# Expert rows loaded three slots ahead in the state-space stage, and 77 and 94 expert blocks in place of 80 and 96

## The chip, the core and the metric

The kernel runs on one core of a Trainium2 chip. The metric is the device time of one execution in microseconds (us); lower is better. The core has five engines that run side by side and wait for each other through semaphores: TensorE (PE), VectorE (DVE), ScalarE (ACT), GpSimd (POOL) and SyncE (SP), which here does nothing but wait and issue transfers. An engine works through its own instructions strictly in order, so a wait in SP's program also holds back every transfer that stands behind it.

## What is computed

Two layers over x of shape (2, 2048, 256), 4096 tokens in all, everything in float32. Layer 0 is a gated linear attention with a dense MLP, then a mixture of experts: each token goes to 2 of 14 experts (hidden 176) beside a shared one. Layer 1 is a state-space block (48 heads of 64, state 128, a causal convolution of four taps over 3072 channels) whose output is added to its input, then a mixture of 16 experts (hidden 96), again 2 for each token:

```
# layer 1, state space, for each token
h = exp(A * dt) * h + B (x) x ;  y = h . C + D * x
out = (rms(y) * silu(z)) @ out_proj.T ;  x = x + out
# experts, for each token t
for e in top2(t): out[t] += w[t, e] * (silu(x[t] @ wg[e].T) * (x[t] @ wu[e].T)) @ wd[e].T
```

In this kernel the experts of both layers are worked out before the state-space stage, and the sums of the second batch half are completed inside that stage.

## The kernel before

**The stages.** `layer0` (attention, MLP, routing of the first experts), `experts` (first mixture), `front` (what the state-space stage needs, and the second routing), `experts1` (second mixture), `ssm` (state space and the last sums). They follow one another with a barrier between.

**Expert blocks.** The routed rows (two for each token) are sorted by expert and each expert's rows are padded to whole blocks of 128. `experts` walks over NB = 80 blocks; `experts1` over 2 × NB1 = 96, 48 for each batch half of 2048 tokens. Which expert a block belongs to is read from a table, so the number of blocks is fixed at build time, and blocks behind the last one with rows in it do work whose result goes to rows that nobody reads. A block is: load of 128 rows (SP), transposes, gate and up projection, transposed hidden rows, down projection (PE), the splits into high and low parts and the gating between them (ACT, DVE), and an indirect DMA that sends the rows home (POOL). Blocks overlap: in a beat k the engines work on block k+2's transposes, block k's projections, block k-1's hidden rows and block k-2's result. While it walks, `experts` also clears the sorted rows of the second mixture (96 transfers of 128 rows from SP, spread over the blocks behind the fourth). In `experts1` the second half of the blocks also carries 16 groups that add the first half's expert rows to the sums, one for every second block from `FIRST = NB1 + 10` on.

**The state-space stage.** It runs N = 192 slots: 8 steps of 512 tokens, and 24 channel tiles in each. In slot k PE projects tile k (lines 63 to 65: bank X first, then bank Z), does the scores and the state update of tile k-1 (L2501, L2509), reads the state of tile k-2 (L2518), projects tile k-4 out (again L63 to L65), and transposes tile k (L2556). DVE does `to_end(k-1)` (L2823), `convolve(k)` (L2755, then three times L2761, on bank X), `gate(k)` (L2767), `silu(k)` (L2772), `scan(k-1)` (eight times L2803), `own_tokens(k-1)` (L2810) and, last of the slot, `state_part(k-2)` (L2817). POOL does L2678 twice and L2684, L2691, L2695, L2705 once each. So L2755 marks the start of a slot on DVE, and below a slot is counted from its L2755 to the next one's. In the slots with t = 4 (k = 28, 52, 76 and so on) DVE first scales and adds the finished step's output (`evacuate`), ahead of L2755, so the slot before (27, 51, 75) is the long one.

**The pieces.** Slots 6 to 37 (K0 = 6, 32 slots) each carry a piece: one of the two expert rows of 128 tokens of the second batch half. PE transposes it into bank X once the taps of this slot are done (`row_turned`, L2526), DVE adds bank X to the sum of these 128 tokens (`row_added`, L2780), and only then may PE project the next slot into bank X. Two pieces (c = 0 and 1) make a unit u of 128 tokens: its sum `part_acc` is loaded before the first and stored after the second.

**SP's program.** It sets the order of the transfers. For each k: `weights_in(k+2)` (L2388), `log_decay(k+2)` (L2393), `since_start(k+1)` (L2401, which waits for `t1` of tile k-2, that is for L2817, DVE's last instruction of slot k), `weights_out(k-1)` (L2405), then `keep_part` (L2429) if the piece of slot k-2 closed a unit, then `expert_row` (L2421 and, for c = 0, L2425) for the piece of slot k+1. Inside `expert_row` the load of the sum waits for the store of the unit two before:

```
done(sp, "row_turned", i - 2)
sp.dma_start(row[:, i % 2], ...)
if c == 0:
    if u >= 2:
        sp.wait_ge(ph[f"part_kept{u % 2}"], u // 2 * 16)
    sp.dma_start(part_acc[:, u % 2], ...)
```

At k = 2u+9 `keep_part(u)` is issued and right behind it, in the same k, the load of unit u+2, which waits for that store to land. The row tiles (two) and the sums (two) lie in columns of the constant table `tab` that this stage no longer uses, so in the profile a row load is `tab<-expert_scratch`, a sum's load `tab<-acc_scratch` and its store `acc_scratch<-tab`.

Of the kernel before, what the change touches and what calls it, by code (L numbers as in the profile page):

```python
# [13 lines left out]
P = 128  # L14
# [13 lines left out]
IN0, SH0, IN1 = 176, 352, 96  # L28
NB, NB1 = 80, 48

HM, PH, NST = 48, 64, 128
# [67 lines left out]
def program(nc, xT, table, gla_w, gla_wo, wbc, moe0, ffn0, moe1, mamba, a_dram, outT):  # L99
    ctx = ExitStack()  # L100
    with ctx:
# [63 lines left out]
        with ExitStack() as own:  # L165
# [5 lines left out]
            experts1(nc, pool, bank, moe1, down_drams[1], sorted1_dram, out1_dram, acc_dram, disp1, home[:, B * T // P:], swdge, x_all, col)  # L171
        ssm(nc, pool, bank, mamba, wi_dram, wo_dram, a_drams, ea_drams, dec_dram, acc_dram, out1_dram, f_dram, outT, st, vec_dram, swdge, col)

# [1098 lines left out]
def experts(nc, pool, bank, moe0, down_dram, sorted_dram, sorted1_dram, out_dram, disp, swdge, col):  # L1272
# [5 lines left out]
    with ExitStack() as own:  # L1278
# [57 lines left out]
        with ExitStack() as blocks:  # L1336
# [18 lines left out]
            def has(n):  # L1355
                return 0 <= n < NB

            def rows(n):
                return slice(n * P, (n + 1) * P)

            BEATS = range(-2, NB + 3)
            NCLEAR = sorted1_dram.shape[0] // P
            with nc.Block(no_gpsimd_drain=True) as block:

                @block.sync
                def _(sp):
                    for n in range(NB):
                        done(sp, "xt", n - RX)
                        done(sp, "spot", n - RX)
                        sp.dma_start(x[:, n % RX], sorted_dram[rows(n)]).then_inc(ph[f"x{n % RX}"], 16)  # L1370
                        if n == RX:
                            sp.wait_ge(ph["zeros"], 1)
                        if n >= RX:
                            m = n - RX
                            for i in range(m * NCLEAR // (NB - RX), (m + 1) * NCLEAR // (NB - RX)):
                                sp.dma_start(sorted1_dram[rows(i)], zeros[:]).then_inc(ph["cleared"], 16)
                    sp.wait_ge(ph["cleared"], NCLEAR * 16)

                @block.gpsimd
                def _(pl):  # L1380
                    for n in range(NB):
                        done(pl, "y", n)
                        pl.indirect_dma_start(out_dram[:], bass.IndirectOffsetOnAxis(ap=home[:, n % RH, :], axis=0),  # L1383
                                              y[:, n % RO], None).then_inc(swdge[f"home0{n % RO}"], 16)
                    for r in range(RO):
                        pl.wait_ge(swdge[f"home0{r}"], NB // RO * 16)

                @block.tensor
                def _(pe):
# [41 lines left out]

                    for k in BEATS:
                        if has(k + 2):
                            turn(k + 2)
                        if has(k):
                            gate_up(k)
                        if has(k + 1) and (k + 1) % EL == 0:
                            n = min(EL, NB - k - 1)
# [92 lines left out]
def front(nc, pool, bank, wbc, acc_dram, rows_out, sorted_dram, f_dram, a_drams, ea_drams, dec_dram, home, disp1, swdge,  # L1531
# [6 lines left out]
    with ExitStack() as own:  # L1538
# [50 lines left out]
        with nc.Block(no_gpsimd_drain=True) as block:  # L1589
# [247 lines left out]
            def _(dve):  # L1837
# [7 lines left out]
                for k in BEATS:  # L1845
# [100 lines left out]
                    if bb is not None:  # L1946
                        done(dve, "ranks", bb)
                        js = slice(bb * NG, (bb + 1) * NG)
                        if bb:
# [7 lines left out]
                               {"place": disp1["place"][:, :, js], "weight": x_all[:, js, D + 2:D + 4].rearrange("p g c -> p c g"),  # L1957
                                "expert": disp1["expert"][:, bb * NB1:(bb + 1) * NB1],
                                "of_block": disp1["of_block"][:, bb * NB1:(bb + 1) * NB1]})
        ph.clear()  # L1960


def experts1(nc, pool, bank, moe1, down_dram, sorted_dram, rows_out, acc_dram, disp1, partition, swdge, x_all, col):
# [4 lines left out]
    GU, HH, Q = 2 * IN1, IN1, 8  # L1968
    N = B * NB1
    NG = NS * NJ  # L1970
# [10 lines left out]
    with ExitStack() as own:  # L1981
# [108 lines left out]
        with nc.Block(no_gpsimd_drain=True) as block:  # L2090

            @block.sync
            def _(sp):
                def expert_rows(u):
                    if u == 0:
                        for n in range(NB1 - RO, NB1):
# [15 lines left out]
                for k in range(-2 - RX, N + 3):  # L2112
                    n = k + 2 + RX
                    if has(n):
                        if n == NB1:
# [114 lines left out]
            def _(pl):  # L2230
# [8 lines left out]
                for r in range(RO):  # L2239
                    pl.wait_ge(swdge[f"home1{r}"], N // RO * 16)  # L2240

# [69 lines left out]

def ssm(nc, pool, bank, m_dram, wi_dram, wo_dram, a_drams, ea_drams, dec_dram, acc_dram, rows_out, f_dram, outT, st, vec_dram, swdge, col):

    with ExitStack() as own:
# [44 lines left out]
        def has(g):  # L2361
            return 0 <= g < N
# [19 lines left out]
        with nc.Block(no_gpsimd_drain=True) as block:  # L2382

            @block.sync
            def _(sp):
# [30 lines left out]
                def expert_row(i):  # L2416
                    u, c = i // 2, i % 2
                    ts = slice(u * P, (u + 1) * P)
                    a = FIRST_ROW + 2 * (T + u * P)
                    done(sp, "row_turned", i - 2)  # L2420
                    sp.dma_start(row[:, i % 2], rows_out[a:a + 2 * P].rearrange("(p c) d -> p c d", c=2)[:, c, :]).then_inc(ph[f"row{i % 2}"], 16)  # L2421
                    if c == 0:
                        if u >= 2:
                            sp.wait_ge(ph[f"part_kept{u % 2}"], u // 2 * 16)
                        sp.dma_start(part_acc[:, u % 2], acc_dram[1, :, :, ts]).then_inc(ph[f"part{u % 2}"], 16)  # L2425

                def keep_part(u):
                    done(sp, "row_added", 2 * u + 1)
                    sp.dma_start(acc_dram[1, :, :, u * P:(u + 1) * P], part_acc[:, u % 2]).then_inc(ph[f"part_kept{u % 2}"], 16)  # L2429

                def sums(s):
                    done(sp, "kept", s - 1, 16)
                    if s == NS:
                        for r in range(2):
                            sp.wait_ge(ph[f"part_kept{r}"], NU // 2 * 16)
                    sp.dma_start(acc[:], acc_dram[s // NS, :, :, step(s)]).then_inc(ph["acc"], 16)
# [19 lines left out]
                sp.dma_start(chain[:, 0], m_dram[:, :, MP_ST:MP_W].rearrange("t p c -> p t c")).then_inc(ph["init"], 16)  # L2456
                for k in range(0, N + 1):
                    if has(k + 2):
                        weights_in(k + 2)
                        log_decay(k + 2)  # L2460
                    if has(k + 1):
                        since_start(k + 1)
                    if has(k - 1):
                        weights_out(k - 1)
                    if piece(k - 2) is not None and piece(k - 2) % 2:
                        keep_part(piece(k - 2) // 2)
                    if piece(k + 1) is not None:
                        expert_row(piece(k + 1))
                    s, t = k // NCT, k % NCT
# [13 lines left out]
            def _(pe):  # L2483
# [37 lines left out]
                def row_turned(k):  # L2521
                    i = piece(k)
                    pe.wait_ge(ph[f"row{i % 2}"], (i // 2 + 1) * 16)
                    done(pe, "tap", k, NR)
                    for h in range(KD):
                        o = pe.transpose(bank[:, X, h * P:(h + 1) * P], row[:, i % 2, h * P:(h + 1) * P], col("ident"))  # L2526
                    o.then_inc(ph["row_turned"], 1)
# [222 lines left out]
            def _(dve):  # L2750
# [23 lines left out]
                def row_added(i):  # L2774
                    u = i // 2
                    if i % 2 == 0:
                        dve.wait_ge(ph[f"part{u % 2}"], (u // 2 + 1) * 16)
                    done(dve, "row_turned", i)
                    done(dve, "row_added", i - 1)
                    dve.tensor_tensor(part_acc[:, u % 2], bank[:, X, 0:D].rearrange("p (k t) -> p k t", k=KD), part_acc[:, u % 2], ALU.add)\  # L2780
                        .then_inc(ph["row_added"], 1)
# [180 lines left out]
```

## Time and profile before

| | us |
|---|---|
| median of 3 executions | 3188.53 (3184.73 to 3191.90) |
| the profiled execution's own time | 3188.92 |
| its span, first to last instruction | 3187.1 |
| PE, DVE, ACT, POOL busy over the span | 2725.0, 2393.8, 2133.6, 1980.3 |

Lines of the profile name the source line, the engine and the tiles (written `out<-in`). In a timeline the first two numbers are the start and the duration in us, and a bracket at the end tells how long the engine stood idle before the instruction and what ended that. "Releaser" is the instruction or transfer for which it waited. SPq is SP's sequencer issuing a transfer. The clock in the rows is the granted clock of TensorE as a share of full speed.

### The profile page before, as it was taken

Reading aid. Unit: us, or ns where it says so; the run is one execution under the profiler, and the core shown is the slowest. Engines: PE = TensorE matmul, PEld = TensorE weight load, DVE = VectorE, ACT = ScalarE, POOL = GpSimd, SP = SyncE. Lnnn points to the kernel's source line nnn. Section 1 sums busy time; section 2 is a strip of 40 time slices with the busy share of each in tenths; the row PEclk is TensorE's granted clock in tenths of the full one; section 3 lists DMA queues with packets and bytes.
Section 4 is the critical chain, followed back from the end, with each engine's and each line's share of the span. In section 5 each row is a group of like instructions: output and inputs, shape, how many; then the busy total and the mean of one; then the engine's idle time right before and its main releaser. Section 6 shows DMA issues by size and latency. Waiting matters only on the chain.

```text
span 3187.1 us, 58909 instructions
## 1 busy us (share of the span) xinstructions
PE 2725.0 (86%) x17390; PEld 2136.2 (67%) x17390; DVE 2393.8 (75%) x6012; ACT 2133.6 (67%) x4702; POOL 1980.3 (62%) x1702
## 2 busy tenths in 40 slices
PE   3699888985569887378788889999999999999998
PEld 2366666654459765277566667788787878878786
DVE  2466666663377588558677778999899999999996
ACT  3454455432255466345576668999899999999996
POOL 2222221216224314554477678999999999999998
PEclk9699998997879998689899999999999999999999
DMA  5455554545656554447765566676766667666663
GB/s 131 111 180 168 170 175 163 183 134 179 201 177 195 173 161 155 148 130 219 216 202 175 171 195 206 199 227 200 241 203 208 218 199 226 201 213 211 197 215 123
DMA packets 321372, 589.70 MB, mean 185 GB/s; under 512 B 48022, under 2 KB 139574, under 8 KB 320566
## 3 DMA queue, kind: packets, MB, share of 16 engines
q1 hardware_dynamic: 306470, 545.73, 55.6%
q0 software_dynamic: 14592, 40.19, 3.4%
q8 instruction: 150, 2.46, 0.3%
q14 instruction: 160, 1.31, 0.1%
HBM read 465.11 MB, written 124.83 MB: 185 GB/s over the span
## 4 chain that ended last, share of the span: by engine, by line
POOL 28%; issue 8%; DMA 5%; DVE 4%; ACT 2%; SPq 2%; PE 1%; POOLq 0%; DVEq 0%; ACTq 0%
POOL mm L2678 6%; POOL y L2691 6%; POOL y_lo L2684 6%; POOL yz L2695 5%; POOL y L2705 5%; DMA tab<-expert_scratch 2%; DMA acc_scratch<-tab 2%; DVE part L2803 2%; SPq L2401 1%; DMA tab<-acc_scratch 1%; ACT mt L2608 1%; DVE t L2817 1%; DVE cv L2761 1%; SPq L2405 1%; DVE t L2810 1%
## 5 line engine op out<-in xcount | busy, mean ns | idle before, releaser
L2678 POOL TENSOR_TENSOR mm<-mt,cb 128x512 f32<-128x512 f32 x384 | 489.6, 1298 | 60.4 <-ACT mt L2628 58.1
L2608 ACT ACTIVATE mt<-a_wide,a_tok 128x128 f32<-128x128 f32 x1536 | 487.0, 389 | 3.5 <-POOL mm L2678 2.8
L2761 DVE SCALAR_TENSOR_TENSOR cv<-bank,taps,cv 128x509 f32<-128x509 f32 (+2 forms) x576 | 429.4, 745 | 13.6
L63 PE MATMUL bank<-f,wi 128*128 128x512 f32 x768 | 324.1, 422 | 17.1 <-DMA wi<-ssm_wi_split 14.1
L64 PE MATMUL bank<-f,wi 128*128 128x512 f32 x768 | 306.4, 399 | 0.0
L65 PE MATMUL bank<-f,wi 128*128 128x512 f32 x768 | 305.9, 398 | 0.0
L2684 POOL TENSOR_TENSOR y_lo<-yz,y_hi 128x512 fp32r<-128x512 f32 x192 | 246.5, 1284 | 77.8 <-ACT y_hi L2633 77.7
L2695 POOL TENSOR_TENSOR yz<-y,zs 128x512 f32<-128x512 f32 x192 | 248.5, 1294 | 15.1
L2691 POOL TENSOR_TENSOR y<-t 128x512 f32<-128x512 f32 x192 | 246.2, 1283 | 0.0
L2705 POOL TENSOR_TENSOR y<-y,ys 128x512 f32<-128x512 f32 x184 | 237.4, 1290 | 2.3 <-ACT ys L2622 2.3
L2501 PE MATMUL bank<-mm,x_tok 128*64 128x128 f32 x3072 | 226.1, 283 | 11.9 <-POOL mm L2678 11.8
L2501 PEld LDWEIGHTS bank<-mm,x_tok 128*64 128x64 f32 x3072 | 161.4, 136 | 100.9 <-issue 67.8
L2628 ACT ACTIVATE mt<-mt 128x512 f32<-128x512 f32 x384 | 221.4, 624 | 5.8
L2509 PE MATMUL bank<-xd,b_tok 128*128 128x128 f32 x1536 | 223.0, 288 | 0.0
L2509 PEld LDWEIGHTS bank<-xd,b_tok 128*128 128x128 f32 x1536 | 186.4, 191 | 33.1 <-issue 33.1
L1383 POOL DMA_INDIRECT expert_scratch<-ex_y,ex_home x80 | 76.6, 957 | 186.2 <-ACT ex_y L1472 185.8
L2803 DVE SCALAR_TENSOR_TENSOR part<-part,dec,bank 128x64 f32<-128x64 f32 x768 | 181.6, 278 | 13.6
L63 PEld LDWEIGHTS bank<-f,wi 128*128 128x128 f32 x768 | 146.9, 191 | 46.5 <-DMA wi<-ssm_wi_split 14.5
L952 POOL TENSOR_TENSOR l_s_out<-l_s_raw,l_s_out 128x768 fp32r<-128x768 f32 x33 | 61.5, 1863 | 186.5 <-ACT l_s_out L803 186.5
L63 PE MATMUL bank<-y_hi,wo 128*128 128x512 f32 x384 | 173.9, 453 | 3.4 <-POOL y_lo L2684 3.4
L65 PEld LDWEIGHTS bank<-f,wi 128*128 128x128 f32 x768 | 146.2, 190 | 36.1
L64 PEld LDWEIGHTS bank<-f,wi 128*128 128x128 f32 x768 | 147.3, 192 | 26.6
(476 smaller groups left out, 8142.3 us busy)
## 6 DMA issues: line engine op xcount, KB each, us to landing
wi<-ssm_wi_split SPq DMA_DIRECT2D x192, 512.0 KB
a_wide<-a_scratch SPq DMA_DIRECT2D x192, 512.0 KB
l_fw<-ffn_split SPq DMA_DIRECT2D x72, 768.0 KB
ea<-ea_scratch SPq DMA_DIRECT2D x384, 128.0 KB
wo<-ssm_wo_split SPq DMA_DIRECT2D x192, 256.0 KB
sorted_scratch<-ex_zeros SPq DMA_DIRECT2D x96, 130.5 KB
ey_x<-sorted_scratch SPq DMA_DIRECT2D x96, 130.5 KB
ssm_wi_split<-l_s_out SPq DMA_DIRECT2D x24, 512.0 KB
```

The costliest lines, as they stand in the source:

```text
L63: pe.matmul(out, wh, xh, start=first, stop=False)
L64: pe.matmul(out, wh, xl, start=False, stop=False)
L65: return pe.matmul(out, wl, xh, start=False, stop=last)
L2501: i = pe.matmul(bank[h * PH:(h + 1) * PH, INTRA, chunk(j)], x_tok[:, j, h * PH:(h + 1) * PH], mm[:, h, chunk(j)], start=True, stop=True)
L2509: i = pe.matmul(bank[:, UPD, chunk(j)], b_tok[:, g // NCT * NJ + j, :], xd[:, j, :], start=True, stop=True)
L2608: i = act.activation(mt[:, h, chunk(j)], a_wide[:, g % R, h, chunk(j)], ACT.Relu, bias=a_tok[:, s * NJ + j, 2 * t + h:2 * t + h + 1], scal ...
L2678: pl.tensor_tensor(mm[:, :, ts], mt[:, :, ts], cb[:, js, :].rearrange("p j t -> p (j t)") .unsqueeze(1).broadcast_to([P, 2, TS // 2]), ALU ...
L2684: pl.tensor_tensor(y_lo[:], yz[:, g % 2], y_hi[:].bitcast(F32), ALU.subtract).then_inc(ph["y_lo"], 1)
L2691: pl.tensor_tensor(y[:], t1[:], t2[:, g % 2], ALU.add).then_inc(ph["y"], 1)
L2695: pl.tensor_tensor(yz[:, g % 2], y[:], zs[:, g % NS], ALU.mult).then_inc(ph["yz"], 1)
L2705: pl.tensor_tensor(y2[:], y2[:], ys[:], ALU.add).then_inc(ph["y2"], 1)
L2761: dve.scalar_tensor_tensor(cv[:, a:TS], bank[:, X, 0:TS - a], taps[:, t, k:k + 1], cv[:, a:TS], ALU.mult, ALU.add).then_inc(ph["tap"], 1)
```

## The change

Two edits. First, in `ssm`: four row tiles and three sum tiles in place of two and two (in other columns of the same table), and in SP's program the loads move to the head of each k: the row of the piece of slot k+3 (its tile must be free of piece k-1), the sum's load for the unit that opens in slot k+2 (it waits for the store of the unit three before), and the store of the unit that the piece of slot k-2 closed; all three stand before `weights_in(k+2)`. Second, in `experts` and `experts1`: the blocks that are walked over become 77 and 2 × 47, from (rows + experts × 127) / 128 rounded down; the tables and the layout of the sorted rows keep their sizes.

```
+USED0, USED1 = (2 * B * T + E0 * (P - 1)) // P, (2 * T + NE * (P - 1)) // P
...
 experts:
-                return 0 <= n < NB
+                return 0 <= n < USED0
...
-                    for n in range(NB):
+                    for n in range(USED0):
...
-                            for i in range(m * NCLEAR // (NB - RX), (m + 1) * NCLEAR // (NB - RX)):
+                            for i in range(m * NCLEAR // (USED0 - RX), (m + 1) * NCLEAR // (USED0 - RX)):
...
-                        pl.wait_ge(swdge[f"home0{r}"], NB // RO * 16)
+                        pl.wait_ge(swdge[f"home0{r}"], (USED0 - r + RO - 1) // RO * 16)
...
 front (tables of the two halves written 47 apart):
-                                "expert": disp1["expert"][:, bb * NB1:(bb + 1) * NB1],
+                                "expert": disp1["expert"][:, bb * USED1:bb * USED1 + NB1],
...
 experts1:
-    N = B * NB1
+    N = B * USED1
...
-            return slice(n * P, (n + 1) * P)
-
-        FIRST, EVERY, LEAD = NB1 + 10, 2, 5
+            a = (n // USED1 * NB1 + n % USED1) * P
+            return slice(a, a + P)
+
+        FIRST, EVERY, LEAD = USED1 + 10, 2, 5
...
 ssm:
-        row = col("scan64").rearrange("p (a d) -> p a d", a=2)
-        part_acc = col("scan128").rearrange("p (a k t) -> p a k t", a=2, k=KD)
+        RR, RP = 4, 3
+        a = _cols["scan64"][0]
+        row = tab[:, a:a + RR * D].rearrange("p (a d) -> p a d", a=RR)
+        part_acc = [tab[:, a:a + D].rearrange("p (k t) -> p k t", k=KD) for a in (_cols[n][0] for n in ("mean", "causal64", "router0"))]
...
-                    done(sp, "row_turned", i - 2)
-                    sp.dma_start(row[:, i % 2], rows_out[...]...).then_inc(ph[f"row{i % 2}"], 16)
-                    if c == 0:
-                        if u >= 2:
-                            sp.wait_ge(ph[f"part_kept{u % 2}"], u // 2 * 16)
-                        sp.dma_start(part_acc[:, u % 2], acc_dram[1, :, :, ts]).then_inc(ph[f"part{u % 2}"], 16)
+                    done(sp, "row_turned", i - RR)
+                    sp.dma_start(row[:, i % RR], rows_out[...]...).then_inc(ph[f"row{i % RR}"], 16)
+
+                def part_in(u):
+                    if u >= RP:
+                        sp.wait_ge(ph[f"part_kept{u % RP}"], u // RP * 16)
+                    sp.dma_start(part_acc[u % RP], acc_dram[1, :, :, u * P:(u + 1) * P]).then_inc(ph[f"part{u % RP}"], 16)
...
                 for k in range(0, N + 1):
+                    if piece(k + 3) is not None:
+                        expert_row(piece(k + 3))
+                    if piece(k + 2) is not None and piece(k + 2) % 2 == 0:
+                        part_in(piece(k + 2) // 2)
+                    if piece(k - 2) is not None and piece(k - 2) % 2:
+                        keep_part(piece(k - 2) // 2)
                     if has(k + 2):
                         weights_in(k + 2)
                         log_decay(k + 2)
...
                     if has(k - 1):
                         weights_out(k - 1)
-                    if piece(k - 2) is not None and piece(k - 2) % 2:
-                        keep_part(piece(k - 2) // 2)
-                    if piece(k + 1) is not None:
-                        expert_row(piece(k + 1))
```

PE's `row_turned` and DVE's `row_added` stay where they are and take the new tile numbers.

## Rows read from the trace of the kernel before

**Rows 1.** The profile's page: chain that ended last, by engine and by line.
```profile
POOL 28%; issue 8%; DMA 5%; DVE 4%; ACT 2%; SPq 2%; PE 1%; POOLq 0%; DVEq 0%; ACTq 0%
POOL mm L2678 6%; POOL y L2691 6%; POOL y_lo L2684 6%; POOL yz L2695 5%; POOL y L2705 5%; DMA tab<-expert_scratch 2%; DMA acc_scratch<-tab 2%; DVE part L2803 2%; SPq L2401 1%; DMA tab<-acc_scratch 1%; ACT mt L2608 1%; DVE t L2817 1%; DVE cv L2761 1%; SPq L2405 1%; DVE t L2810 1%
```
**Rows 2.** Busy time by stretch: slots 6 to 37, 102 to 133, slot 28.
```profile
core 0: us, PE busy (x) PEld busy (x) DVE busy (x) ACT busy (x) POOL busy (x), PEclk, DMA share, GB/s
1601.85:1939.37 337.52, 275.02 (x1796) 221.12 (x1795) 248.02 (x579) 234.91 (x549) 244.74 (x206) 0.95 0.61 185
2449.65:2701.75 252.10, 249.00 (x1732) 202.37 (x1731) 237.23 (x547) 232.87 (x549) 244.02 (x207) 1.00 0.70 217
1835.16:1843.13 7.97, 7.95 (x59) 6.51 (x56) 7.70 (x20) 6.93 (x18) 7.68 (x8) 1.00 0.69 186
```
**Rows 3.** Waits in slots 6 to 37: total us, times, longest.
```profile
POOL y_lo L2684 <- ACT y_hi L2633: 73.7, 28, 6.3
...
PE bank L2526 <- DMA tab<-expert_scratch: 59.5, 30, 3.3
...
DVE tab L2780 <- DMA tab<-acc_scratch: 45.7, 13, 5.3
...
DVE tab L2780 <- PE bank L2526: 28.4, 18, 2.5
```
**Rows 4.** The chain in order of time, two slots: start, us, what.
```profile
1661.09 0.45 SPq L2401
...
1662.85 3.34 DMA acc_scratch<-tab
1666.20 2.44 DMA tab<-acc_scratch
...
1672.29 0.47 SPq L2401
...
1674.07 3.31 DMA tab<-expert_scratch
1677.37 0.04 issue
1677.42 0.45 PE bank L2526 x2
...
1681.51 0.45 SPq L2401
```
**Rows 5.** Timeline: slot 28's piece on PE and DVE; starts of slots 123 and 124.
```profile
1837.79 0.38 PE L2526 MATMUL bank<-tab 128*128 128x128 f32 x2
...
1838.97 0.43 DVE L2780 TENSOR_TENSOR tab<-bank,tab 128x256 f32<-128x256 f32 x1
...
1839.77 0.48 PE L63 MATMUL bank<-f,wi 128*128 128x512 f32 x1
...
2612.50 0.22 DVE L2755 SCALAR_TENSOR_TENSOR cv<-bank,taps,first 128x3 f32<-128x3 f32 x1
...
2624.83 0.21 DVE L2755 SCALAR_TENSOR_TENSOR cv<-bank,taps,first 128x3 f32<-128x3 f32 x1
```
**Rows 6.** Timeline of SP's issues: around a unit's change, then without a piece.
```profile
1661.09 1.09 SPq L2401 DMA_DIRECT2D ea<-ea_scratch  x2
1662.22 0.58 SPq L2405 DMA_DIRECT2D wo<-ssm_wo_split  x1
1662.85 0.57 SPq L2429 DMA_DIRECT2D acc_scratch<-tab  x1
1663.47 0.61 SPq L2421 DMA_DIRECT2D tab<-expert_scratch  x1
1666.20 0.55 SPq L2425 DMA_DIRECT2D tab<-acc_scratch  x1
1666.80 0.60 SPq L2388 DMA_DIRECT2D wi<-ssm_wi_split  x1
...
2559.37 0.43 SPq L2388 DMA_DIRECT2D wi<-ssm_wi_split  x1
2559.84 0.43 SPq L2393 DMA_DIRECT2D a_wide<-a_scratch  x1
```
**Rows 7.** Timeline: slot 118's first projection; chain in order of time: the stage's first weights.
```profile
2571.47 0.48 PE L63 MATMUL bank<-f,wi 128*128 128x512 f32 x1
...
1546.12 5.95 DMA wi<-ssm_wi_split
```
**Rows 8.** Expert blocks by one instruction: first mixture; 13 blocks of the second.
```profile
L1459 ACT ACTIVATE ex_th<-bank x80: 310/311/318, 908.5 to 1083.7; 128x176 f32<-128x176 f32 x80
...
1418.80 0.24 ACT L2205 ACTIVATE ey_th<-bank 128x96 f32<-128x96 f32 x1
...
1443.50 0.24 ACT L2205 ACTIVATE ey_th<-bank 128x96 f32<-128x96 f32 x1
...
L2205 ACT ACTIVATE ey_th<-bank 128x96 f32<-128x96 f32 x13 | 3.2, 244 | 0.0
```
**Rows 9.** SP's waits over the whole span, in the first mixture's line.
```profile
SPq L1353 <- DVE ex_spot L244: 82.9, 71, 2.0
```

More of the change, by code:

```diff
@@ L171, in program @@
             experts1(nc, pool, bank, moe1, down_drams[1], sorted1_dram, out1_dram, acc_dram, disp1, home[:, B * T // P:], swdge, x_all, col)
-        ssm(nc, pool, bank, mamba, wi_dram, wo_dram, a_drams, ea_drams, dec_dram, acc_dram, out1_dram, f_dram, outT, st, vec_dram, swdge, col)
+        ssm(nc, pool, bank, mamba, wi_dram, wo_dram, a_drams, ea_drams, dec_dram, acc_dram, out1_dram, f_dram, outT, st, vec_dram, swdge, tab, col)
 def places(dve, p, n0, E, NG, one, pick, comb, ranks, sums, tmp, past, numbers, count, found, base, out):
@@ L1355, in has @@
             def has(n):
-                return 0 <= n < NB
+                return 0 <= n < USED0
             def rows(n):
                 return slice(n * P, (n + 1) * P)
-            BEATS = range(-2, NB + 3)
+            BEATS = range(-2, USED0 + 3)
             NCLEAR = sorted1_dram.shape[0] // P
@@ L1380, in _ @@
                 def _(pl):
-                    for n in range(NB):
+                    for n in range(USED0):
                         done(pl, "y", n)
@@ L1437, in _ @@
                         if has(k + 1) and (k + 1) % EL == 0:
-                            n = min(EL, NB - k - 1)
+                            n = min(EL, USED0 - k - 1)
                             _, v = nc.values_load_multi_w_load_instructions(disp["expert"][0:1, k + 1:k + 1 + n],
@@ L1957, in _ @@
                                {"place": disp1["place"][:, :, js], "weight": x_all[:, js, D + 2:D + 4].rearrange("p g c -> p c g"),
-                                "expert": disp1["expert"][:, bb * NB1:(bb + 1) * NB1],
-                                "of_block": disp1["of_block"][:, bb * NB1:(bb + 1) * NB1]})
+                                "expert": disp1["expert"][:, bb * USED1:bb * USED1 + NB1],
+                                "of_block": disp1["of_block"][:, bb * USED1:bb * USED1 + NB1]})
         ph.clear()
@@ L2095, in expert_rows @@
                     if u == 0:
-                        for n in range(NB1 - RO, NB1):
+                        for n in range(USED1 - RO, USED1):
                             sp.wait_ge(swdge[f"home1{n % RO}"], (n // RO + 1) * 16)
@@ L2114, in _ @@
                     if has(n):
-                        if n == NB1:
+                        if n == USED1:
                             sent(sp, 1)
@@ L2239, in _ @@
                 for r in range(RO):
-                    pl.wait_ge(swdge[f"home1{r}"], N // RO * 16)
+                    pl.wait_ge(swdge[f"home1{r}"], (N - r + RO - 1) // RO * 16)
             @block.vector
@@ L2309, in router_tiles, with ssm @@
     return t
-def ssm(nc, pool, bank, m_dram, wi_dram, wo_dram, a_drams, ea_drams, dec_dram, acc_dram, rows_out, f_dram, outT, st, vec_dram, swdge, col):
+def ssm(nc, pool, bank, m_dram, wi_dram, wo_dram, a_drams, ea_drams, dec_dram, acc_dram, rows_out, f_dram, outT, st, vec_dram, swdge, tab, col):
     with ExitStack() as own:
@@ L2417, in expert_row @@
                     u, c = i // 2, i % 2
-                    ts = slice(u * P, (u + 1) * P)
                     a = FIRST_ROW + 2 * (T + u * P)
-                    done(sp, "row_turned", i - 2)
-                    sp.dma_start(row[:, i % 2], rows_out[a:a + 2 * P].rearrange("(p c) d -> p c d", c=2)[:, c, :]).then_inc(ph[f"row{i % 2}"], 16)
-                    if c == 0:
-                        if u >= 2:
-                            sp.wait_ge(ph[f"part_kept{u % 2}"], u // 2 * 16)
-                        sp.dma_start(part_acc[:, u % 2], acc_dram[1, :, :, ts]).then_inc(ph[f"part{u % 2}"], 16)
+                    done(sp, "row_turned", i - RR)
+                    sp.dma_start(row[:, i % RR], rows_out[a:a + 2 * P].rearrange("(p c) d -> p c d", c=2)[:, c, :]).then_inc(ph[f"row{i % RR}"], 16)
+                def part_in(u):
+                    if u >= RP:
+                        sp.wait_ge(ph[f"part_kept{u % RP}"], u // RP * 16)
+                    sp.dma_start(part_acc[u % RP], acc_dram[1, :, :, u * P:(u + 1) * P]).then_inc(ph[f"part{u % RP}"], 16)
                 def keep_part(u):
                     done(sp, "row_added", 2 * u + 1)
-                    sp.dma_start(acc_dram[1, :, :, u * P:(u + 1) * P], part_acc[:, u % 2]).then_inc(ph[f"part_kept{u % 2}"], 16)
+                    sp.dma_start(acc_dram[1, :, :, u * P:(u + 1) * P], part_acc[u % RP]).then_inc(ph[f"part_kept{u % RP}"], 16)
                 def sums(s):
@@ L2433, in sums @@
                     if s == NS:
-                        for r in range(2):
-                            sp.wait_ge(ph[f"part_kept{r}"], NU // 2 * 16)
+                        for r in range(RP):
+                            sp.wait_ge(ph[f"part_kept{r}"], (NU - r + RP - 1) // RP * 16)
                     sp.dma_start(acc[:], acc_dram[s // NS, :, :, step(s)]).then_inc(ph["acc"], 16)
@@ L2522, in row_turned @@
                     i = piece(k)
-                    pe.wait_ge(ph[f"row{i % 2}"], (i // 2 + 1) * 16)
+                    pe.wait_ge(ph[f"row{i % RR}"], (i // RR + 1) * 16)
                     done(pe, "tap", k, NR)
                     for h in range(KD):
-                        o = pe.transpose(bank[:, X, h * P:(h + 1) * P], row[:, i % 2, h * P:(h + 1) * P], col("ident"))
+                        o = pe.transpose(bank[:, X, h * P:(h + 1) * P], row[:, i % RR, h * P:(h + 1) * P], col("ident"))
                     o.then_inc(ph["row_turned"], 1)
@@ L2776, in row_added @@
                     if i % 2 == 0:
-                        dve.wait_ge(ph[f"part{u % 2}"], (u // 2 + 1) * 16)
+                        dve.wait_ge(ph[f"part{u % RP}"], (u // RP + 1) * 16)
                     done(dve, "row_turned", i)
                     done(dve, "row_added", i - 1)
-                    dve.tensor_tensor(part_acc[:, u % 2], bank[:, X, 0:D].rearrange("p (k t) -> p k t", k=KD), part_acc[:, u % 2], ALU.add)\
+                    dve.tensor_tensor(part_acc[u % RP], bank[:, X, 0:D].rearrange("p (k t) -> p k t", k=KD), part_acc[u % RP], ALU.add)\
                         .then_inc(ph["row_added"], 1)
```

## The prediction

> **What bounds the kernel now.** I read the chain of waits first. POOL's five operations of the state-space stage fill most of it, but three transfers stand in it too, and all three belong to the expert rows: the row load and the sum's store at 2% each, the sum's load at 1% [rows 1]. These exist only in slots 6 to 37, so I cut the busy times there and in a stretch of the same shape without pieces. Slots 102 to 133 are in the same position of their steps (102 is 6 plus four steps of 24), so they hold the same edge operations and one long slot behind a step's end, as slots 6 to 37 do. The two stretches of 32 slots took 337.52 and 252.10 us: 10.55 and 7.88 us a slot [rows 2]. The difference, 85.4 us, is what the pieces cost today. In the stretch without pieces PE is busy for 249.0 of 252.1 us, POOL for 244.0 and DVE for 237.2: three engines are close to full. In the other one PE is busy for 275.0 of 337.5, no engine is near full, and the granted clock is 0.95 against 1.00 [rows 2].
>
> The waits of that stretch name the cause: PE waits 59.5 us for row loads, DVE 45.7 us for the sums' loads and 28.4 us for the transposes that PE could not start. POOL's 73.7 us behind ACT are the far end of the same delay [rows 3]. The chain in order of time shows the loop. SP waits for DVE's last instruction of the slot (L2817), issues L2401 and L2405, and only then the row that is needed in the running slot: it lands 3.31 us later, the two transposes take 0.45 us and DVE goes on. In every second slot it is the sum: the store takes 3.34 us, and the load that waits for it 2.44 us [rows 4]. From 1661.09 to 1681.51 this is 20.4 us for two slots, 10.2 us a slot, so this loop alone explains most of the 10.55.
>
> **The change, part by part.**
>
> Row loads. The load of slot k+3's row is issued where SP stood before with its step k-1 finished. Its wait is for the transposes of piece k-1; SP's step k-1 had already waited for L2817 of slot k-1, behind them in DVE's order, so this wait ends nothing. The lead becomes about three slots, over 23 us, against 3.31 us to land [rows 4]. The 59.5 us of PE's waits and the 28.4 us behind them go.
>
> Sums. The load for slot k+2 waits for the store of three units before, which SP issued one step earlier: some 7.9 us ago, against 3.34 us to land [rows 4]. Then it has two slots for 2.44 us. The 45.7 us go too. The store now waits for an addition of slot k-2, long done.
>
> What stays. Two transposes on PE (0.38 us) and an addition on DVE (0.43 us) in each of 32 slots. The trace of before has one piece that nothing waited for, in slot 28, because the long slot ahead of it gave its row time to land. There the transposes and the addition carry no wait, and PE's next projection starts 0.37 us behind the addition's end (1839.77 against 1838.97 plus 0.43) [rows 5]. This slot took 7.97 us, with DVE busy for 7.70, PE for 7.95 [rows 2]. It is the nearest row to what every piece slot becomes. 31 slots at 7.97 make 247.1 us. The long slot 27 takes what slot 123 takes, at the same place of its step, 2624.83 - 2612.50 = 12.3 us [rows 5], and 0.4 for the addition: 12.7. Sum 259.8 us, a saving of 77.7.
>
> Bounds: if the pieces' work is wholly hidden beside POOL, the stretch falls to 252.1 us (saving 85.4). If transposes and addition stand in series in each slot, it is 252.1 + 32 × (0.45 + 0.43) = 280.3 us (saving 57.2). I take 259.8, because it is measured on a piece slot of this very kernel. It assumes full clock; slot 28 had 1.00, and PE will have no long gap in the stretch.
>
> SP and its queue. SP's step without a piece needs 2.5 us of issues (1.09 + 0.58 + 0.43 + 0.43), a piece adds one issue or two more, 0.6 us each [rows 6]; a slot leaves 7.9. They are moved ahead of the weights of slot k+2. These have 2571.47 - 2559.37 = 12.1 us from issue to first use today [rows 6, 7], and the longest landing that the chain shows is 5.95 us, at the stage's start [rows 7]. A delay of 1.2 us there costs nothing. In the closing steps the weights even leave earlier: today they wait 2.7 us for the sum (1663.47 to 1666.20) [rows 6].
>
> Expert blocks. The first mixture's 80 blocks start from 908.5 to 1083.7: 175.2 / 79 = 2.22 us each [rows 8]. Three fewer save 6.7 us. The clearing transfers now share 73 blocks in place of 76; SP waits 82.9 us in that loop [rows 9], which covers four per cent more transfers a block. The second mixture's steady blocks took (1443.50 - 1418.80) / 13 = 1.90 us [rows 8]; two fewer save 3.8 us. Nothing else hangs on the dropped blocks: the groups move one block earlier with them. Bounds: 0 and twice this, since the first half's blocks are uneven. I take 10.5 us.
>
> Sum: 77.7 + 10.5 = 88.2 us. Against the profiled execution's 3188.92 this gives 3100.7; it stands 0.4 above the median of 3188.53, so the forecast is 3101 us.
>
> **A rule set against the rows.** The store, the sum's load and the row load took 3.34, 2.44 and 3.31 us for 128 KB or less of data each, 9.1 us in the two-slot loop [rows 4]. The Trainium skill, DMA: Bandwidth & Descriptors, section Anatomy of one DMA, gives some 2.0 us plus the bytes over 436e3 for a transfer; my estimate from it is 2.3 us each, 6.9 in the loop. With those prices the loop would be 2.2 us shorter, the wait removed 35 us smaller over 16 units, and the forecast near 3136. The measured stretch of 337.5 us holds the longer landings, so the rows decide.
>
> **The rivals.**
>
> The DMA engines set the pace. The stretch moved 337.52 us × 185 GB/s = 62.4 MB; in 260 us this is 240 GB/s, above the 217 of the stretch without pieces [rows 2]. If 217 were the ceiling, it would take 287.8 us and the kernel 3188.9 - 49.7 - 10.5 = 3129. Against it: the DMA share at 217 GB/s was only 0.70 [rows 2]. The Trainium skill, on the same page, section Issuing engines are not separate DMA queues, says that all transfers share the same 16 engines, whoever issues them.
>
> In series. Bank X is the place: PE can't project the next slot into it before DVE has read the row. If DVE reaches the addition before PE has done the transposes, or PE the projection before the addition, the cost is the upper bound above: 3188.9 - 57.2 - 10.5 = 3121. Against it: the 0.37 us of room and no wait in slot 28 [rows 5].
>
> The waits were covered. If the slots are held by an engine and not by the transfers, only the blocks count: 3188.9 - 10.5 = 3178. That is also what comes if the change does not do what it says, that is, if SP reaches the earlier loads no sooner. Against it: slot 28 did the same work in 7.97 us. The Trainium skill, Perfetto Trace Analysis, section Identifying the Most-Contended Engine, would have one lighten the engine with the highest occupancy first, and the first edit lightens none.
>
> Slower. The weights of slot k+2 stand behind the row, the sum and its store on SP's queue. If they land late, PE waits at L63 in every piece slot. It decides from the point where a slot exceeds 10.55 + 10.5 / 32 = 10.9 us: with a lead of 12.1 - 1.2 = 10.9 us, and a slot that grows with the landing, the weights must take some 14 us to land. At 16 us the slots take about 13 us: 3188.9 + 32 × 2.4 - 10.5 = 3255. Against it: 5.95 us with everything in flight at once [rows 7].
>
> **How the numbers follow.** The forecast's case gets 0.76; its own range is 3093 to 3112, from all hidden to a third of the way towards series. DMA pace 0.09, in series 0.09, covered 0.03, slower 0.02, and 0.01 for a stretch unchanged with no gain from the blocks. The range from 3092 to 3123 takes in the forecast's case and the series case and leaves out 0.15. A measurement of this kernel can tell some 0.2%, 6.4 us, from no change. Faster has the first four cases, 0.97; within 0.2% 0.01; slower 0.02.
>
> **What would show it.** Slots 6 to 37 at about 8 us each and the stretch near 260 us; no row for waits on `tab<-expert_scratch` or `tab<-acc_scratch`; DVE above 95% busy there and the clock at 1.00; block pitches unchanged at 2.22 and 1.90 us with 77 and 94 blocks. A wait at L2780 behind L2526, or at L63 behind L2780, would speak for the series case; at L63 behind `wi` for the DMA cases. The forecast is wrong if the stretch takes over 270 us.

## The result, and the profile after

The changed kernel takes 3096.3 us (median of 4, 3090.8 to 3113.9) against 3190.2 for the kernel before beside it: a ratio of 0.971 with a 95% interval of 0.967 to 0.976. The profiled execution took 3097.3 us with a span of 3095.5. The forecast was 3101.

In the changed kernel DVE's taps are L2761 and L2767 (L2755 and L2761 before), PE's transposes of a row L2532, the addition L2786, SP's row load L2424, the sum's load L2429, its store L2433, its issues of `ea` L2405 and of `wo` L2409. Lines 63 to 65 are now 64 to 66.

The page's chain that ended last, by engine and by line, against [rows 1]:

```profile
POOL 35%; issue 10%; ACT 3%; DVE 2%; POOLq 1%; PE 1%; DMA 0%; SPq 0%; ACTq 0%; DVEq 0%
POOL mm L2684 8%; POOL y L2697 7%; POOL yz L2701 7%; POOL y_lo L2690 6%; POOL y L2711 6%; ACT mt L2614 1%; DVE cv L2767 1%; POOLq L2360 1%; ACT ys L2628 0%; ACT mt L2634 0%; DVE bank L2838 0%; ACT L2649 0%; POOL first L2726 0%; DMA wi<-ssm_wi_split 0%; DVE xd L2829 0%
```

The transfers of rows and sums, 5% of the chain before, have left it; POOL's five operations took their place. The busy times of slots 6 to 37, against [rows 2]:

```profile
core 0: us, PE busy (x) PEld busy (x) DVE busy (x) ACT busy (x) POOL busy (x), PEclk, DMA share, GB/s
1587.33:1842.78 255.45, 253.65 (x1796) 210.10 (x1795) 245.67 (x578) 232.52 (x549) 245.42 (x206) 1.00 0.80 243
```

The same 32 slots now take 255.45 us in place of 337.52, with PE busy for 99% of it, DVE and POOL for 96% each, and the clock at 1.00 in place of 0.95. The slots alternate between 7.81 and 7.91 us. The largest waits there, against [rows 3]:

```profile
engine line waited for: us in total, times, longest us
PEld bank L2507 <- issue: 11.3, 31, 0.4
ACT halo L2598 <- PE bank L66: 10.8, 29, 0.4
ACT bank L2623 <- DVE cv L2767: 8.8, 32, 1.0
```

No wait for `tab<-expert_scratch` or `tab<-acc_scratch` is left in that answer. SP's issues of two steps, against [rows 6]:

```profile
1712.70 1.10 SPq L2405 DMA_DIRECT2D ea<-ea_scratch  x2
1713.84 0.58 SPq L2409 DMA_DIRECT2D wo<-ssm_wo_split  x1
1714.47 0.43 SPq L2424 DMA_DIRECT2D tab<-expert_scratch  x1
1714.94 0.56 SPq L2429 DMA_DIRECT2D tab<-acc_scratch  x1
1715.55 0.60 SPq L2392 DMA_DIRECT2D wi<-ssm_wi_split  x1
1716.19 0.43 SPq L2397 DMA_DIRECT2D a_wide<-a_scratch  x1
1720.61 1.09 SPq L2405 DMA_DIRECT2D ea<-ea_scratch  x2
1721.75 0.58 SPq L2409 DMA_DIRECT2D wo<-ssm_wo_split  x1
1722.38 0.43 SPq L2424 DMA_DIRECT2D tab<-expert_scratch  x1
1722.85 0.58 SPq L2433 DMA_DIRECT2D acc_scratch<-tab  x1
1723.48 0.60 SPq L2392 DMA_DIRECT2D wi<-ssm_wi_split  x1
```

The transfers still leave at the same place of DVE's slot, right behind `wo`. What changed is the slot that they serve, and that SP issues the weights without a stop between. The block walks, one instruction a block, against [rows 8]; the third row is the second mixture of the kernel before:

```profile
L1460 ACT ACTIVATE ex_th<-bank x77: 311/312/317, 906.4 to 1074.7; 128x176 f32<-128x176 f32 x77
L2207 ACT ACTIVATE ey_th<-bank x94: 243/245/267, 1321.8 to 1522.1; 128x96 f32<-128x96 f32 x94
```

```profile
L2205 ACT ACTIVATE ey_th<-bank x96: 244/244/262, 1331.6 to 1536.7; 128x96 f32<-128x96 f32 x96
```

The span by parts, from the first and last rows of each walk and the slots' starts (us):

| | before | after | loads only | blocks only |
|---|---|---|---|---|
| first mixture's walk | 175.2 | 168.3 | 175.3 | 168.2 |
| second mixture's walk | 205.2 | 200.3 | 203.3 | 201.6 |
| slots 6 to 37 | 337.5 | 255.5 | 255.7 | 334.1 |
| from slot 38 to the end | 1247.8 | 1252.8 | 1249.5 | 1250.2 |
| span | 3187.1 | 3095.5 | 3111.9 | 3185.7 |

Of the 91.6 us of span, 82.1 came from the pieces' slots and 11.8 from the walks; 2.9 more lie in the stages ahead of and between them, where nothing was changed; 5.0 were lost behind slot 38 and 0.2 in slots 0 to 5. The last two columns are the first two experiments.

### The profile page after: what moved, and what is told of

Same layout as the page of the kernel before. It is cut to its first block, busy times and chain, and to the rows that moved or that the text cites. A ratio compares the mean times of both kernels' runs of the same rounds, so it can differ in the third digit from the quotient of the medians.

```text
span 3095.5 us, 58605 instructions
## 1 busy us (share of the span) xinstructions
PE 2693.5 (87%) x17318; PEld 2112.8 (68%) x17318; DVE 2383.3 (77%) x5972; ACT 2125.2 (69%) x4682; POOL 1976.0 (64%) x1697
## 3 DMA queue, kind: packets, MB, share of 16 engines
q8 instruction: 149, 2.44, 0.3%
## 4 chain that ended last, share of the span: by engine, by line
POOL 35%; issue 10%; ACT 3%; DVE 2%; POOLq 1%; PE 1%; DMA 0%; SPq 0%; ACTq 0%; DVEq 0%
POOL mm L2684 8%; POOL y L2697 7%; POOL yz L2701 7%; POOL y_lo L2690 6%; POOL y L2711 6%; ACT mt L2614 1%; DVE cv L2767 1%; POOLq L2360 1%; ACT ys L2628 0%; ACT mt L2634 0%; DVE bank L2838 0%; ACT L2649 0%; POOL first L2726 0%; DMA wi<-ssm_wi_split 0%; DVE xd L2829 0%
## 5 line engine op out<-in xcount | busy, mean ns | idle before, releaser
L2767 DVE SCALAR_TENSOR_TENSOR cv<-bank,taps,cv 128x509 f32<-128x509 f32 (+2 forms) x576 | 429.7, 746 | 13.6
L2701 POOL TENSOR_TENSOR yz<-y,zs 128x512 f32<-128x512 f32 x192 | 249.0, 1297 | 15.1
```

Of the source, the lines that this page charges most:

```text
L2701: pl.tensor_tensor(yz[:, g % 2], y[:], zs[:, g % NS], ALU.mult).then_inc(ph["yz"], 1)
L2767: dve.scalar_tensor_tensor(cv[:, a:TS], bank[:, X, 0:TS - a], taps[:, t, k:k + 1], cv[:, a:TS], ALU.mult, ALU.add).then_inc(ph["tap"], 1)
```

## The experiments

**1. The two edits apart.** First the stage as changed with the old numbers of blocks:

```
-USED0, USED1 = (2 * B * T + E0 * (P - 1)) // P, (2 * T + NE * (P - 1)) // P
+USED0, USED1 = NB, NB1
```

> 80 and 96 blocks as before, the state-space stage as changed. If the two edits are independent, slots 6 to 37 take 255 to 256 us as in the changed kernel, the block walks 175 and 205 us as before, and the kernel is 80 to 84 us faster than before. If part of the gain in the stage came from the stages ahead of it (another clock or phase at its start), the stretch lies above 260 us.

It took 3113.2 us, ratio 0.975 (0.971 to 0.978); slots 6 to 37 took 255.7 us and the walks 175.3 and 203.3. That is 76.3 us faster by the medians, below the 80 to 84 expected: the stretch gave its 81.8 us, but in this profile the first walk began 3.9 us and the second another 2.7 us later than before, in stages that the edit does not touch. Then the new numbers with `ssm` as before:

> 77 and 94 blocks, the state-space stage as before. Independent edits: the walks take some 168.5 and 200.5 us, 11 to 12 us less together, slots 6 to 37 some 337 us, the kernel 8 to 15 us faster. If a dropped block costs nothing because it has no rows that count, under 5 us.

It took 3181.2 us, ratio 0.996 (0.994 to 0.998). The walks took 168.2 and 201.6 us, 10.6 us less together (11 to 12 expected), and the kernel gained 8.4 us by the medians. Slots 6 to 37 took 334.1: their code is that of the kernel before, which took 337.5, so this stretch differs by some 3 us from one profile to another. Each part of the table goes with its own edit. The medians' gains, 76.3 and 8.4, add up to 84.7, 9 us short of the 93.9 of both; the untouched stages can hide as much, for the first walk began between 900.6 and 917.4 us in the thirteen profiles. The second walk is uneven: over the eleven kernels profiled here with 94 blocks it took 197.7 to 204.3 us, mean 201.4, and 205.2 and 203.3 in the two with 96. So the first walk's saving of 6.9 us is firm (77 blocks took 167.9 to 169.0 in all eleven), the second's is near 3 us, uncertain by about as much.

**2. Rows late, sums late.** The changed kernel with one kind put back each time. The kernels of this experiment and of the next two ran once each, so they are read by their stretch. Rows late:

```
                 for k in range(0, N + 1):
-                    if piece(k + 3) is not None:
-                        expert_row(piece(k + 3))
...
                         weights_out(k - 1)
+                    if piece(k + 1) is not None:
+                        expert_row(piece(k + 1))
```

> The changed kernel with the row loads alone put back (row of slot k+1, behind L2409 of step k); the sums' loads stay early. If the row loop of before was complete by itself (L2817, two issues, 3.3 us to land, transposes, the rest of DVE's slot), every piece slot takes 9.2 to 9.3 us: the stretch some 297 us. If the sums made the loss and the rows only stood beside it, under 275 us.

Slots 6 to 37 took 308.4 us. Three waits of that stretch:

```profile
PEld bank L2532 <- DMA tab<-expert_scratch: 46.9, 27, 5.0
DVE tab L2786 <- PE bank L2532: 46.6, 27, 5.3
PE bank L2532 <- DMA tab<-expert_scratch: 41.7, 27, 4.8
```

Sums late:

```
-        RR, RP = 4, 3
+        RR, RP = 4, 2
...
-                    if piece(k + 2) is not None and piece(k + 2) % 2 == 0:
-                        part_in(piece(k + 2) // 2)
-                    if piece(k - 2) is not None and piece(k - 2) % 2:
-                        keep_part(piece(k - 2) // 2)
...
                         weights_out(k - 1)
+                    if piece(k - 2) is not None and piece(k - 2) % 2:
+                        keep_part(piece(k - 2) // 2)
+                    if piece(k + 1) is not None and piece(k + 1) % 2 == 0:
+                        part_in(piece(k + 1) // 2)
```

> The changed kernel with the sums put back (two sum tiles; store, then the load that waits for it, behind L2409 of the step ahead of the unit); the rows stay early. Every second slot should take 11.2 us as before and the others 7.9, less what POOL and ACT had in hand: the stretch 295 to 308 us, the wait at the addition for the sum's load 35 us or more. If rows and sums hid each other, under 275 us.

Slots 6 to 37 took 314.3 us; the typical pair was 11.2 and 7.8 us. Two of its waits:

```profile
DVE tab L2786 <- DMA tab<-acc_scratch: 52.9, 15, 6.7
...
PE bank L64 <- DVE tab L2786: 38.2, 14, 5.6
```

The second row tells how DVE's wait spreads: PE may not project the next slot into bank X before the row is out of it. Rows alone bring back 53.0 of the 82.1 us and sums alone 58.9. They overlap in the slots that need both, so undoing either brings back well over half of the loss. Both were longer than expected. Rows late exceeded its 297 us by 11; slots 6 and 8 took 12.1 and 12.0 us and slot 34 15.1. Sums late exceeded the upper end of its range by 6; slots 30, 32 and 34 took 13.1, 12.5 and 14.9 us in place of 11.2. Why was not followed further.

**3. Place or lead.** What is needed: three slots of lead with more tiles, or only that the loads stand ahead of SP's wait for DVE's last instruction? Two tiles of each kind as before, the same slots' loads in each step k as before, but at its head and no longer at its end:

```
-        RR, RP = 4, 3
+        RR, RP = 2, 2
...
                 for k in range(0, N + 1):
-                    if piece(k + 3) is not None:
-                        expert_row(piece(k + 3))
-                    if piece(k + 2) is not None and piece(k + 2) % 2 == 0:
-                        part_in(piece(k + 2) // 2)
                     if piece(k - 2) is not None and piece(k - 2) % 2:
                         keep_part(piece(k - 2) // 2)
+                    if piece(k + 1) is not None:
+                        expert_row(piece(k + 1))
+                    if piece(k + 1) is not None and piece(k + 1) % 2 == 0:
+                        part_in(piece(k + 1) // 2)
                     if has(k + 2):
                         weights_in(k + 2)
```

> Two row tiles and two sum tiles as before, loads of slot k+1 as before, but issued at the head of SP's step k (store first, then row, then sum), ahead of the step's wait for L2817 and not behind it. Theory position: the place ahead of that wait gives each load one slot more, 9 us for a landing of 3.3, and 8.0 us for store and load in series against 11.7: slots 6 to 37 take 255 to 260 us with no more tiles than before. Theory lead: the three slots and the added tiles are needed, and the stretch takes over 280 us.

265.1 us: 72.4 of the 82.1 us come from the place alone. Between the two ranges, but nearer to the first; 9.7 us are missing. SP's waits in that stretch, in this run and then in the changed kernel:

```profile
SPq L2429 <- DMA acc_scratch<-tab: 76.8, 14, 7.6
SPq L2405 <- DVE t L2823: 46.7, 19, 6.0
```

```profile
SPq L2405 <- DVE t L2823: 115.3, 32, 7.4
```

SP stood 76.8 us before the sums' loads until the stores had landed, with the weights of slot k+2 behind it. Four timeline rows of this run show the longest kind, 8.85 us from the store's issue to the load's:

```profile
1660.24 0.57 SPq L2433 DMA_DIRECT2D acc_scratch<-tab  x1
1660.86 0.61 SPq L2424 DMA_DIRECT2D tab<-expert_scratch  x1
1669.09 0.55 SPq L2429 DMA_DIRECT2D tab<-acc_scratch  x1
1669.68 0.60 SPq L2392 DMA_DIRECT2D wi<-ssm_wi_split  x1
```

That left two readings: the late weights, or too few tiles. The same kernel with the three calls behind `weights_in` and `log_decay`, still ahead of the wait for L2823:

> As the run with two tiles each, but store, row and sum are issued behind the weights (L2392, L2397) of step k, still ahead of the wait for L2817. There SP stood 76.8 us waiting for stores to land, with the weights behind it, and the stretch took 265.1 us. If those late weights made the 10 us over 255.4, the stretch takes 255 to 258 us here. If two tiles are too few for themselves (rows or sums late), it stays at 263 us or more.

273.6 us, worse. SP still waited 70.2 us for stores, and with the weights out of the way the rows stood behind that wait:

```profile
PE bank L2532 <- DMA tab<-expert_scratch: 12.5, 8, 4.3
DVE tab L2786 <- DMA tab<-acc_scratch: 12.5, 5, 6.2
```

In eight places SP also waited for a row tile to come free, 5.6 us in all; the two waits were not separated. So late weights alone were not the cause: in this order rows and sums are late. The third kernel takes the wait away by its cause, with a third sum tile (RR, RP = 2, 3) in the first order:

> As the run with two tiles each, at the head of the step, with a third sum tile, so that the sum's load waits for an older store; rows with two tiles and a lead of one slot. If the wait for the store made the 10 us, the stretch takes 255 to 257 us and PE has no wait for a row. If a lead of one slot is too short for the rows, it lies above 260 us with waits at L2532 for tab<-expert_scratch.

257.3 us, with SP's wait for stores gone and one wait of 1.0 us for a row. It gives 80.2 of the 82.1 us, so what the two-tile kernel lacked was nearly all the third sum tile. The last 1.9 us lie in slots 34 and 35 (8.5 and 9.1 us), behind the step in which SP waits for the output's store; the changed kernel, with two more row tiles and the longer lead, has no long slot there.

**4. What sets 7.86 us.** The changed kernel with one engine's share of a piece made larger. The rows have the columns of the stretch's row in the section on the result. A second addition on DVE, into a tile nobody reads:

> The changed kernel with a second addition of 128x256 on DVE in each piece slot (into a tile that nobody reads), 0.34 us of DVE's time. If DVE sets the pace of the piece slots, they go from 7.86 to some 8.2 us and the stretch from 255.4 to 265 to 267 us. If POOL or PE sets it, under 258 us.

```profile
1592.76:1857.06 264.30, 261.53 (x1805) 210.94 (x1803) 254.95 (x611) 229.71 (x550) 244.96 (x207) 1.00 0.77 235
```

The transposes done twice:

> The changed kernel with the two transposes of each piece done twice, 0.25 us more of PE's time a slot. If PE sets the pace, the stretch is 8 us longer, 263 us; if DVE sets it and PE has that room ahead of the addition, under 258 us.

```profile
1590.03:1851.89 261.86, 260.26 (x1860) 216.98 (x1859) 247.33 (x578) 232.60 (x549) 245.62 (x206) 1.00 0.78 238
```

One more POOL operation (it took 0.405 us; the stretch's POOL time grew by 8.6 us, 0.27 a slot):

> The changed kernel with one more POOL operation (128x128, some 0.35 us) at the end of each piece slot. If POOL sets the pace, the stretch is 11 us longer, 266 us; if DVE sets it and POOL has 0.2 us of room in each slot, 255 to 261 us.

```profile
1590.29:1851.26 260.97, 257.58 (x1796) 209.47 (x1795) 247.20 (x579) 233.72 (x549) 254.06 (x238) 1.00 0.78 238
```

Over 255.45 us these are 8.9, 6.4 and 5.5 us more, 0.28, 0.20 and 0.17 us a slot. All three fall between the branches or at their edge: DVE's 264.3 lies just under its 265 to 267, PE's 261.9 just under its 263, and POOL's 261.0 at the upper end of "has room". What each run added to its engine's own program is in the traces. For PE, the changed kernel and then the run with double transposes:

```profile
1716.52 0.38 PE L2532 MATMUL bank<-tab 128*128 128x128 f32 x2
1716.65 0.48 PE L64 MATMUL bank<-y_hi,wo 128*128 128x512 f32 x1
...
1714.64 0.60 PE L2532 MATMUL bank<-tab 128*128 128x128 f32 x4
1714.99 0.48 PE L64 MATMUL bank<-y_hi,wo 128*128 128x512 f32 x1
```

From the first transpose to PE's next matmul 0.13 us became 0.35. The slots of 7.81 and 7.91 us became 8.04 and 8.13, so these 0.22 us came back whole. PE sets the pace of the ordinary piece slots, which agrees with its 99% busy time. The second addition moved DVE's next work by 0.33 us and cost 0.28: DVE is some 0.05 us a slot behind PE. POOL's 0.27 us cost 0.17, so it is some 0.1 us behind. The page's chain, which names POOL most, does not tell this. By estimate the transposes' 0.13 us in each of 32 slots make 4.2 us and the shorter long slot takes back 0.4; the stretch is 3.4 us longer than the one without pieces.

Do transposes, addition and projection stand in series through bank X? In the changed kernel they do not:

```profile
1713.33 2.31 DVE L2767 SCALAR_TENSOR_TENSOR cv<-bank,taps,cv 128x509 f32<-128x509 f32 x3
1716.99 0.42 DVE L2786 TENSOR_TENSOR tab<-bank,tab 128x256 f32<-128x256 f32 x1
1718.49 0.48 PE L64 MATMUL bank<-f,wi 128*128 128x512 f32 x1
```

The transposes start 0.88 us behind the taps' end, the projection 1.08 us behind the addition's. With the second addition both fall to 0.15 us in most slots: there bank X has become the limit.

**5. A slot that varies.** From slot 38 on the changed kernel's profile is 5.0 us longer, 3.2 of them in slot 78, which took 13.4 us (10.2 before, 9.9 to 14.6 in the experiments above, 7.7 and 7.8 in its neighbours). That the change made it slower is not shown: the run with the loads alone has the same stage and took 9.9. Behind the load of the second half's initial states, 1.5 MB in one transfer, SP needs 6.83 us to issue the next weights, and PE waits for them. The kernel before has the same: 6.80 us for that issue, and a wait of PE of 2.2 us. Changed kernel, timeline of SP, then of PE:

```profile
2156.26 0.67 SPq L2449 DMA_DIRECT2D chain<-mamba_dram  x1
2156.97 6.83 SPq L2392 DMA_DIRECT2D wi<-ssm_wi_split  x1
2163.84 0.45 SPq L2397 DMA_DIRECT2D a_wide<-a_scratch  x1
...
2170.76 0.79 PE L64 MATMUL bank<-f,wi 128*128 128x512 f32 x1 [4.09 <-DMA wi<-ssm_wi_split]
```

The load cut into eight, one a step:

```
+        NI = 8
...
-                def start():
+                def start(i):
...
-                    sp.dma_start(chain[:, 0], m_dram[:, :, MP_ST:MP_W]...).then_inc(ph["init"], 16)
+                    ts = slice(i * NCT // NI, (i + 1) * NCT // NI)
+                    sp.dma_start(chain[:, 0, ts], m_dram[ts, :, MP_ST:MP_W]...).then_inc(ph["again"], 16)
...
-                    if k == (NS - 1) * NCT + 4:
-                        start()
+                    if 0 <= k - (NS - 1) * NCT - 4 < NI:
+                        start(k - (NS - 1) * NCT - 4)
```

PE and DVE wait for all eight at slot 96.

> The changed kernel with the 1.5 MB load of the second batch half's initial states (chain<-mamba_dram, issued at k = 76, needed at slot 96) cut into 8 loads of three tiles, one a step from k = 76 on. Slot 78 took 13.4 us in the changed kernel and 10.2 before, against 7.7 for its neighbours, and PE waited 4.1 us there for wi. If the one large load holds back the weights behind it on SP's queue, slot 78 falls to 7.7 to 8 us and the part of the stage behind slot 38 by 2 to 6 us, the kernel by 0.1 to 0.2% against the changed one. If it is the start of the second half that costs there, slot 78 stays above 10 us.

Slot 78 took 7.8 us and the part from slot 38 on 1246.2 us, 6.6 less than in the changed kernel. The next weights' issue fell from 6.83 us (6.1 to 7.7 in the twelve profiles with the one large load) to 0.98:

```profile
2155.93 0.64 SPq L2451 DMA_DIRECT2D chain<-mamba_dram  x1
2156.62 0.98 SPq L2393 DMA_DIRECT2D wi<-ssm_wi_split  x1
```

The kernel took 3091.7 us (median of 6, 3090.0 to 3098.5), ratio to the kernel before 0.971 (0.969 to 0.973). It beats the kernel before; against the changed one, whose ratio is the same within its interval, only the profile tells it apart.

## Why the prediction was right

The direction, the size (94 us of medians against 88) and the range held. The closeness of the total is in part luck. In the two profiles the span fell by 91.6 us against 88.2: the slots gave 4.4 more than forecast and the blocks 1.3, and three differences for which the sum had no term, 2.9 us gained ahead of and between the stages and 5.0 and 0.2 lost, nearly cancel. The untouched stages alone differ by more from one profile to another.

**The waits.** All three named by [rows 3] are gone, and experiment 2 gives each kind its price. The reading of [rows 4] as a loop through SP's wait for DVE's last instruction is shown by experiment 3: with no more tiles than before, the place ahead of that wait returned 72.4 us. The prediction spoke of the lead of three slots; that was more than was needed. Its second half, that the store of three units before has landed, was the part that counted beside the place: with two sum tiles the store's landing stood in SP's way.

**What stays.** Taken: 7.97 us a slot, from slot 28 of before, and 12.7 for the long one, 259.8 in all. Measured: 7.86 on average and 11.9 for slot 27, 255.45. The long slot was 0.4 us shorter than slot 123, not 0.4 longer. This term was 4.4 us too high; the pieces' own work is hidden nearly whole, 3.4 us over the 252.1 of the stretch without pieces. The prediction spoke of work hidden beside POOL; experiment 4 shows PE at the pace of these slots, with DVE and POOL within 0.1 us of it. Why slot 28 itself took 7.97 us before and 7.81 after was not tested. The prediction's own range is described as a third of the way towards series; its upper end of 3112 is more than half of the way, a third would be 3108.

**The blocks.** 6.7 and 3.8 us forecast; 6.9 measured for the first, and about 3 for the second by the means, 4.9 between the two profiles.

**SP and its queue.** "A delay of 1.2 us there costs nothing" held: no wait for `wi` is among the stretch's. The slower rival's mechanism exists, though: in experiment 3, where SP stood before the weights, PE waited 2.9 us for `wi` in that stretch, and slot 78 shows it with a large transfer in front. The order in the changed kernel avoids it.

**The other rivals.** The DMA engines as the pace: the stretch now moves 243 GB/s, above the 217 taken as a ceiling, at a share of 0.80. Series: experiment 4 finds 0.88 and 1.08 us of room around bank X in the changed kernel. It was near, though: 0.33 us more of DVE's time a slot used this room up. Covered waits: refuted by experiment 1.

**The page's price for a transfer.** By the 2.0 us plus bytes of DMA: Bandwidth & Descriptors (the Trainium skill), section Anatomy of one DMA, the forecast would have been 3136, outside the measured range. That section gives its figure for transfers that GpSimd issues; SP issued these. The store and the row load took 3.34 and 3.31 us [rows 4] against the 2.3 estimated from it, the sum's load 2.44, so what was removed was larger.

**Not foreseen.** The 5.0 us behind slot 38: the prediction took this part as fixed, while slot 78 varies by 4.6 us from one profile to another.

## What to carry to other kernels

A queue that issues in order turns every wait in its program into lateness for all that stands behind it: look at what each prefetch is queued behind before adding buffers. One slot of place gave 72 us here, one more tile 8, all further lead 2. Where a load must wait for a store of the same ring, give the ring one tile more than the overlap needs, so that the issuing engine never stops at that wait; and cut a large one-off load into small pieces: 192 KB worked here, the only size tried, beside loads of 128 to 512 KB.

## What the runs showed of the hardware

The same transfer's landing time depended on the order of the issues. The store of a sum landed in 3.4 us (median) in the changed kernel and in 7.1 us with two tiles each, where SP issued several transfers at once after each stop; the rows took 3.7 and 6.6 us, the sum's load, on the contrary, 4.1 in the changed kernel and 2.5 with two tiles, where it left right behind the stop. The mean rates were close, 243 and 235 GB/s. That bunching is the cause was not tested by itself. And an issue is not always short: behind 1.5 MB in one transfer the next one held SP for 6.83 us, behind 192 KB for 0.98.
